# A decoder layer whose attention scores are computed a second time with the keys on the partitions

## What is computed

```
x = _layernorm(x + _attn(x, x, x, sa_wq, ..., True), ln1_g, ln1_b)
x = _layernorm(x + _attn(x, enc, enc, ca_wq, ..., False), ln2_g, ln2_b)
x = _layernorm(x + _moe(x, router_w, router_b, e_w1, e_b1, e_w2, e_b2), ln3_g, ln3_b)
# _attn: scores = Q K^T / sqrt(16) (+ causal mask); a = softmax(scores); o = a V; o @ wo + bo
```

## Time and profile before

| | us |
|---|---|
| device time, median of 3 runs | 861.68 |
| lowest and highest | 849.74, 862.56 |
| span of the profiled execution | 852.4 |

### The profile page before, as it was taken

How to read it: one execution, slowest core, us unless ns; L and a number is a source line. 1 busy time by engine, 2 the same in 40 slices (tenths; PEclk the granted TensorE clock), 3 DMA queues, 4 the chain that set the end, 5 groups by cost and what they waited for, 6 DMA issues and landing times.

```text
span 852.4 us, 17248 instructions
## 1 busy us (share of the span) xinstructions
PE 719.4 (84%) x5304; PEld 576.1 (68%) x5305; DVE 422.8 (50%) x1047; ACT 402.6 (47%) x1656; POOL 182.7 (21%) x208
## 2 busy tenths in 40 slices
PE   4494959879889898798997879968999999999953
PEld 3273736646657566576565667957999999999942
DVE  2343636747666567575485563532333333333227
...
GB/s 126 201 205 159 103 116 96 64 130 118 80 138 66 131 96 63 132 113 95 111 57 42 119 107 172 192 200 206 47 56 54 51 56 56 56 56 56 32 209 99
DMA packets 126391, 90.89 MB, mean 107 GB/s; under 512 B 26240, under 2 KB 122032, under 8 KB 126352
## 3 DMA queue, kind: packets, MB, share of 16 engines
...
q10 hardware_dynamic: 576, 0.53, 0.2%
...
HBM read 66.58 MB, written 23.80 MB: 106 GB/s over the span
## 4 chain that ended last, share of the span: by engine, by line
PE 52%; DMA 13%; issue 10%; DVE 9%; ACT 8%; POOL 4%; SPq 3%; ACTq 0%; DVEq 0%; POOLq 0%
PE bank L840 15%; PE bank L823 15%; DMA w<-q_parts 7%; ACT probs L1052 3%; PE bank L750 3%; DMA q_parts<-w 2%; PE bank L777 2%; PE bank L738 2%; PE bank L731 2%; PE bank L748 2%; PE bank L792 2%; PE bank L705 2%; DVE nmax L1387 2%; POOL w L490 2%; PE bank L770 2%
## 5 line engine op out<-in xcount | busy, mean ns | idle before, releaser
L1052 ACT ACTIVATE probs<-bank,nmax 128x77 f32<-128x77 f32 (+2 forms) x512 | 184.3, 382 | 130.9 <-DVE nmax L1387 122.5
L995 ACT ACTIVATE shared<-bank,b 128x128 f32<-128x128 f32 x312 | 84.9, 383 | 176.8 <-PE bank L823 176.7
L1387 DVE TENSOR_REDUCE nmax<-bank 128x4 f32<-128x308 f32 (+2 forms) x160 | 96.0, 601 | 105.7 <-PE bank L738 100.6
L840 PE MATMUL bank<-w,shared 128*128 (+1 forms) x624 | 143.7, 384 | 0.6 <-issue 0.6
L840 PEld LDWEIGHTS bank<-w,shared 128*128 128x128 f32 x624 | 117.6, 193 | 15.8 <-issue 0.9
L823 PEld LDWEIGHTS bank<-shared,w_cross 128*128 128x128 f32 x992 | 115.6, 192 | 1.6
L823 PE MATMUL bank<-shared,w_cross 128*128 128x128 f32 x992 | 115.8, 275 | 0.0
L1052 ACT ACTIVATION_READ_ACCUMULATOR probs<-bank,nmax 128x1 f32 x512 | 109.3, 213 | 0.0
L1136 POOL DMA_INDIRECT expert_rows<-shared x39 | 38.1, 977 | 247.0 <-DVE shared L1343 247.0
L731 PE MATMUL bank<-causal,identb 128*128 128x512 bf16 x96 | 42.6, 444 | 54.9 <-DMA w<-q_parts 53.6
L1393 DVE COPY w<-bank 128x512 f32<-128x512 f32 (+1 forms) x112 | 76.0, 679 | 7.4 <-PE bank L750 6.1
...
## 6 DMA issues: line engine op xcount, KB each, us to landing
...
shared<-dispatched SPq DMA_DIRECT2D x39, 129.0 KB, 2.1
...
```

The source lines that it names most:

```text
L840: last = nc.tensor.matmul(y_of(n), gT[n % 2][:, f, :], w2[:, e, f, :], start=f == 0, stop=f == FC - 1)
L995: last = nc.scalar.activation(gT[n % 2][:, f, :], h_bank[n % 2][f // 4][:, f % 4 * P:f % 4 * P + P], ACT.Gelu, bias=b1[:, bass.ds(e * FC + ...
L1052: last = nc.scalar.activation(p[:, a * keys:a * keys + keys], s_bank[u.bank][:, a * keys:a * keys + keys], ACT.Exp, bias=nmax[u.bank][:, a ...
L1387: v.tensor_reduce(nmax[u.bank][:, 0:n], s_bank[u.bank][:, 0:n * keys].rearrange("p (h k) -> p h k", h=n), AX, ALU.max, negate=True).then_i ...
```

## The change

What it does:

- Scores are computed twice. The first time (`s1A`, `s1B`, queries on the partitions, as before) only for the maxima, which DVE writes for all heads of a batch (`nm`). Then `mxA`/`mxB`: DVE splits the negated maxima into three bf16 parts; `rA`/`rB`: PE turns them, ACT copies them (`nrows`), SP puts them by three DMAs as rows 96 to 98 under the stacked q (`stack_max`), over against three rows of ones in the stacked k. The second time (`s2A`, `s2B`) keys are on the partitions, and the product has the maximum already subtracted. ACT takes one exponential of a whole unit of 512 columns, without bias or sum, straight into `probsT`. There are no turned probabilities, no copies of them and no sums.
- v has 32 columns a head, column 16 being one, so that the matmul with v gives the sums too. Groups of four heads (`pvA`, `pvB`); the output has the values on the partitions (`oS`, copied by ACT), is turned back (`oX`, PE), divided by the sums (DVE), and turned again (`oT`) for wo.
- Units a batch: 12 first and 12 second ones for A, 6 first and 8 second ones for B.
- Two stacks for q and for k, filled in turns; q and k of batch f, maxima and s1A of batch a, values of the last group and cross-attention's start of batch b, cross-attention's end and router of batch p: f = t+1, a = t, b = t-1, p = t-2. The order is written out by hand as a list (`TURN`, `TURN_8`, `TURN_9`), all turns unrolled, without a loop.
- Two banks each for first scores, second scores, other work and output.
- x and ctx arrive already turned, and weights lie in DRAM in the order of the partitions (w1 and w2 8 KB in a row for a partition), biases in one array; q's bias and scaling are on ACT. xT, cT, x_in and the transposes of biases are gone.
- w2 of no expert is loaded during the turns (its place holds stacks and probabilities); all eight come after, of them four behind the last early blocks (before: three). w1 of the last expert is loaded in TURN_8.
- The later blocks, their loops and the tail are the same.

The diff, cut to its core:

```diff
+TURN = """
+rB p ; q f ; k f ; s1A a 0 ; s1A a 1 ; pvA b 3 ; oSA b 1 ; qM f ; kM f ; s1A a 2 ; s1A a 3 ; oXA b 1 ; s1A a 4 ;
+s2B p 0 ; s1A a 5 ; s2B p 1 ; oTA b ; vA a ; s1A a 6 ; s2B p 2 ; woA b ; nA b ; s2B p 3 ; pvB p 0 ; s1A a 7 ; s2B p 4 ; s1A a 8 ;
+zA b ; s2B p 5 ; pvB p 1 ; oSB p 0 ; s1A a 9 ; x1T b ; s2B p 6 ; s1A a 10 ; q2 b ; s2B p 7 ; s1A a 11 ; mxA a ; q2M b ; oXB p 0 ;
+pvB p 2 ; pvB p 3 ; oSB p 1 ; k2 b ; rA a ; k2M b ; oXB p 1 ; v2 b ; oTB p ; xres a ;
+woB p ; nB p ; x1res b ; s2A a 0 ; s2A a 1 ; s2A a 2 ; s2A a 3 ; zB p ; s2A a 4 ; pvA a 0 ; x2T p ; s2A a 5 ; s2A a 6 ; route p ; s2A a 7 ; pvA a 1 ; oSA a 0 ; gate p ;
+s2A a 8 ; s1B b 0 ; s2A a 9 ; oXA a 0 ; rank p ; s1B b 1 ; s2A a 10 ; s1B b 2 ; pvA a 2 ; s2A a 11 ; s1B b 3 ; s1B b 4 ; s1B b 5 ; mxB b
+"""
+TURN_8 = """
+table 0 ; rB p ; s2B p 0 ; pvA b 3 ; oSA b 1 ; s2B p 1 ; oXA b 1 ; s2B p 2 ; oTA b ; s2B p 3 ; pvB p 0 ; woA b ; nA b ; eW 0 ; eT 0 ; s2B p 4 ; s2B p 5 ; pvB p 1 ; oSB p 0 ;
+s2B p 6 ; zA b ; s2B p 7 ; eU 0 ; x1T b ; q2 b ; q2M b ; oXB p 0 ; pvB p 2 ; pvB p 3 ; oSB p 1 ; k2 b ; k2M b ; eT 1 ; eW 1 ; oXB p 1 ; v2 b ; eU 1 ; oTB p ; eD 0 ; woB p ; nB p ; x1res b ; eW 2 ; eT 2 ;
+zB p ; eU 2 ; x2T p ; route p ; gate p ; eD 1 ; rank p ; eT 3 ; eW 3 ; s1B b 0 ; s1B b 1 ; s1B b 2 ; s1B b 3 ; s1B b 4 ; s1B b 5 ; mxB b ; eU 3 ; eD 2 ; rB b ; eT 4 ; eW 4 ; eD 3
+"""
+TURN_9 = """
+s2B p 0 ; s2B p 1 ; s2B p 2 ; s2B p 3 ; pvB p 0 ; s2B p 4 ; s2B p 5 ; pvB p 1 ; oSB p 0 ; s2B p 6 ; s2B p 7 ; pvB p 2 ; oXB p 0 ; pvB p 3 ; oSB p 1 ; eU 4 ;
+oXB p 1 ; oTB p ; eT 5 ; eW 5 ; woB p ; nB p ; x1res b ; eD 4 ; zB p ; eU 5 ; x2T p ; route p ; gate p ; eD 5 ; rank p ; eT 6 ; eW 6 ; eU 6 ; later 0 ; pads 0 ; eT 7 ; eW 7 ; eD 6 ; eU 7 ; eT 8 ; eW 8
+"""
...
+        qS, kS, q2S = [stack_at(0), stack_at(2)], [stack_at(1), stack_at(3)], stack_at(4)
...
+            def stack_max(kind, b):
+                to = qS[b % 2] if kind == "A" else q2S
+                sp.wait_ge(nrows_ready[kind], b + 1)
+                for a in range(PARTS):
+                    sp.dma_start(to[KROWS + a:KROWS + a + 1, :, :], nrows[kind][a * H:a * H + H, :]).then_inc(max_stacked[kind], 16)
...
+            for turn in range(0, B):
+                a, f, b, p = turn, turn + 1, turn - 1, turn - 2
+                if p >= 0:
+                    stack_max("B", p)
+                if f < B:
+                    stack(f, "q", "k")
+                stack_max("A", a)
+                if b >= 0:
+                    sp.wait_ge(x1_ready, a)
+                    load_x(a)
+                    stack(b, "q2", "k2")
...
-            def turn(u):
-                pe.wait_ge(probs_ready, u.done)
...
-                    if u.kind == "A":
-                        last = nc.tensor.transpose(o[:, j * P:j * P + P], p[:, j * P:j * P + P], ident[:, :])
...
+            def first_scores(s, kind):
+                if s.n >= 2:
+                    pe.wait_ge(max_ready, s.n - 1)
...
+            def second_scores(s, kind):
+                if s.n >= 2:
+                    pe.wait_ge(probs_ready, s.n - 1)
...
+                if s.m == 0:
+                    pe.wait_ge(max_stacked[kind], MAX_ROWS * (s.b + 1))
...
+                    te.matmul(o_, identb[:, :], causalT[:, None, 0:qn].to_broadcast([P, n, qn]), start=True, stop=False)
...
+                for a, h in enumerate(heads):
+                    last = te.matmul(o[0:keys, a * qn:a * qn + qn], k_[0:KMAX, h, kt * P:kt * P + keys], q_[0:KMAX, h, q0:q0 + qn],
+                                     start=kind == "B", stop=kind == "B" or a == n - 1)
...
+                        last = te.matmul(o[VW * i:VW * i + VW, c0:c0 + S], vz[:, 0, h, :], half_[:, i % 2 * S:i % 2 * S + S], start=True, stop=False)
...
+            def queries_back(s, kind):
+                o = open_bank(s)
+                pe.wait_ge(copied, COPIED[kind, s.b, s.m])
+                for q in range(QT_N):
+                    for g in range(2):
+                        last = te.transpose(o[:, (2 * q + g) * P:(2 * q + g) * P + P], oS[s.m][:, g, q * P:q * P + P], ident[:, :])
...
-                    for a, s_ in enumerate(heads):
-                        h = head_of(c, s_)
-                        last = nc.scalar.activation(p[:, a * keys:a * keys + keys], s_bank[u.bank][:, a * keys:a * keys + keys], ACT.Exp,
-                                                    bias=nmax[u.bank][:, a:a + 1], accum_out=sums[u.kind][:, q, h:h + 1])
...
+                    sc.activation(probsT[s.n % PB][0:keys, :], second_bank[s.n % 2][0:keys, :], ACT.Exp).then_inc(probs_ready, 1)
...
+                own.link(v.tensor_copy(p(0), nm[k][:, :, :]))
+                own.link(v.tensor_tensor(nleft[k][:, :, :], nm[k][:, :, :], p(0), ALU.subtract))
+                own.link(v.tensor_copy(p(1), nleft[k][:, :, :]))
+                v.tensor_tensor(p(2), nleft[k][:, :, :], p(1), ALU.subtract).then_inc(nparts_ready[k], 1)
...
+                    own.link(v.reciprocal(rec[s.m][:, :], o[:, :, HD]))
+                    for q in range(QT_N):
+                        n = 2 * HG
+                        ins = v.tensor_tensor(o_n[:, q, s.m * P:s.m * P + P].rearrange("p (a x) -> p a x", x=HD), o[:, q * n:q * n + n, 0:HD],
+                                              rec[s.m][:, q * n:q * n + n, None].to_broadcast([P, n, HD]), ALU.mult)
```

1203 lines of the change are left out of this document (543 added, 660 removed), and 8 rows, old and new, of tables (BESIDE, EARLY_STEPS).

## The result

| | before | after |
|---|---|---|
| device time, median of 4 runs, us | 856.89 | 881.28 |
| lowest and highest | 849.74, 862.56 | 879.76, 890.29 |
| span of the profiled execution | 852.4 | 877.9 |
| busy PE, DVE, ACT | 719.4, 422.8, 402.6 | 689.5, 370.0, 309.7 |

The ratio is 1.033 (95% interval 1.022 to 1.043). PE, DVE and ACT work less and the kernel takes longer (POOL is as before: 182.3 us for 182.7). The forecast was 833.6 with a range of 786 to 872, so it was wrong in sign and size.

The account below looks back on a forecast made before the run. PE was taken as the bound, with idle time and half clock. 407.5 us to the end of turn 7, 138 for the last turns and 278.8 unchanged gave 824.3; plus 9.3 from span to median, 833.6 us, range 786 to 872.

Parts of the forecast that it names:

- The last two turns: From the end of turn 7 to block 8: 77 us of PE work plus 61 of waits, 138 us, bounds 120 and 152.
- PE's work falling by 3 us only: Steady turn: PE's work goes from 42.3 to 39.0 us, since the second scores and new transposes nearly replace what goes.
- ACT's exponentials: Exponentials of 512 columns in the attention turns: 0.67 us each, bounds 0.48 and 0.95.
- The turns: Steady turns 2 to 6: 50 us at full clock, 11 idle, plus 2 for half clock: 52 us, bounds 46 and 57.
- a chain behind woB: End of a steady turn: norm, router and reductions in sequence take 17.5 us against 10.9 of PE work.
- the term for half clock: Steady turn: the nearly empty last 4 us lower the clock, so q and k run at half of it, 2 us.
- The double stacks: Starts of self scores: two stacks each for q and k, made a batch ahead, remove 34.7 us of waits.
- rival (4): Starts of self scores: double stacks don't free them because parts come too late; 34.7 us stay, 868; chance 0.06.
- The landing of the maxima: DMA of the maxima ahead of the second scores A: taken as 4 us, just hidden, bounds 2.1 and 10.8.
- rival (3): Second scores: maxima land late behind stack loads in SP's queue, 68 us more, 902; chance 0.11.
- The first turns: Turns 0 and 1, filling the pipeline: first scores at 31.5 us, then 22.5 us and 45 us.
- First scores: Start of batch 0's self scores: at 31.5 us for 32.3 before, through the same DMAs.

Follow-up runs that it names:

- e3: The changed kernel with the last two turns' steps and SyncE's loads there reordered, same work; median 837.0 us, ratio 0.979 to the kernel before.
- e2: The changed kernel with unread bf16 matmuls added ahead of TensorE waits, before every rB and in the last two turns; median 852.9 us, ratio 0.995 to before.
- e8: The changed kernel with turn 0's maxima and xT load ahead of stack loads, dummy rows in turn 2, ones rows written later; 865.7 us, 1.014 of before.
- e11: e9 plus ten unread matmuls ahead of the x2T wait in the turns; median 798.3 us, ratio 0.930 to the kernel before.
- e15: e11 with the router's gate and rank moved into the next turn, rank behind the splitting of q and k; median 790.3 us, 0.927 of before.
- e9: The kernel with all repairs together, plus k2 projected and stacked early and q2's DMAs moved ahead; median 808.2 us, ratio 0.943 to before.

## Why the prediction was wrong

The step that failed is the price of filling and of draining the pipeline. The last two turns were put at 138 us with no term for half clock and took 153.3 with about 22 us of it; the first two were put at 67.5 us behind the first scores (22.5 and 45) and took 91.6. That is 39 of the 53.6 us. That order and clock are what costs there is shown for the last turns (e3: 41 us less with the same work, e2: 13.5 less with more work), for the first in part (e8: 9 of 28).

**What bounds the kernel.** PE's work falling by 3 us only, DVE and ACT no bound: right. PE is busy 44.3 us in a turn of after, with the clock at 0.90, DVE 29.1 and ACT 24.6 (28 each were forecast).

**ACT's exponentials.** 0.67 us was an estimate; they take 0.595 for 128x512 (mean of 96). It had no part in the miss.

**The turns.** 52 us were forecast, 53.1 measured, and with them a gain of 3.3 us a batch over before (forecast 4.4). The mechanism was right: a chain behind woB, and a low clock. Mis-sized was the term for half clock. I put the pause at the very end of the turn, over q and k, for 2 us; the trace has it also ahead of x2T and in the middle. Counted as busy time times clock, turns 2 to 6 of after have 39.5 us of work (39.0 forecast), 9.7 idle (11) and 4.4 of half clock (2): idle time too long and half clock too short, so part of the nearness is luck. The sum itself doesn't close either: the waits that it lists for a turn make 12.9 us, not 11. e11 prices the half clock behind x2T at 10 us of the whole, 4.4 of them in the turns themselves, and e15 another order on DVE and POOL at 7 more.

**The double stacks.** Right: 34.7 us of waits for q's and k's stack are gone, and rival (4) with them. But a wait of the same kind took its place: q2 and k2 have one stack each and the same round trip through DRAM, 19.5 us over seven turns. The forecast had it in turn 1 only.

**The landing of the maxima.** Taken as 4 us, with 8.5 as the point from which rival (3) decides. In the steady turns s2A hardly waits: the three rows land in 1.8 us (median of 24), close to the fixed part of about 2.0 us that the Trainium skill gives for DMAs issued by GpSimd ("DMA: Bandwidth & Descriptors", section "Anatomy of one DMA"); these are SyncE's. In turn 0 they took 9 to 10 us from their issue, and were issued 1 to 3.5 us behind their copy. So rival (3) was right in one turn of eight. What failed here is the sentence that the stack loads are through before nrows is ready: it holds in a steady turn (252.9 for the last stack load, 256.9 for nrows of batch 4), and in turn 0 the last of them lands at 61.5, 12 us behind nrows.

**The first turns (28 us, the largest miss).** This is where the sum was thin. First scores: the memset of the ones rows (two of 3.5 us on DVE ahead of the splitting of batch 0) was in the diff and costed at nothing. The start lay 3.7 us over the forecast; without the memsets ahead of it it is 31.0 to 33.6, so some 2 us are theirs. Turn 0: s1A took 11.7 for 8.5, since vA's 2.4 us at low clock were left out; then 15.3 for 6.5 to the first s2A; then 10.5 for 7.5. Turn 1: 54.1 for 45, with 5.9 us for k2's stack and a clock of 0.69 in its second half. e8 gives 9 of the 28 back by order alone, and with k2 early and q ahead of rB turn 1 ends at 108.5 to 111.5 (e9 and the kernels made from it). The remaining 10 to 12 were not taken apart.

**The last turns.** The forecast had 77 us of work and 61 of waits. The two rows above have 51.7 us of busy PE at a clock of 0.77 and 60.9 at 0.83: 112.6 us, about 90 at full clock (39.8 + 50.5), and 43 of idle time. The waits were over-counted by 18 (those listed make 57.9, not 61), the work under-counted by 13, and the 22 us between 90 and 112.6, half clock, not counted at all. In the steady turns a term for half clock was in the sum; in these two, with pauses of 2 to 5 us all over them, there was none.

**The sign.** The forecast of 138 us for a stretch where before needs 102.4 was made from a hand count of waits, and its upper bound, 152, was 1 us short. The first turns had no bounds of their own. Only with one as wide as the miss itself (28 us) and the upper bounds of the others (54 a turn, 152) would the range have ended at 886. The 9.3 us between span and median came out as 3.4, which took 6 us off the miss. That part of the miss is one of method: the steady turn, followed step by step, came out 3% short, the last two, from a count of waits, 10%, and the first two, taken in a line each, 22% (126.8 for 99).
